# A graph layer on one core: gathered groups placed by a table of cycles, and the addition of b2 to x moved behind the last block multiply

## The chip, the core and the metric

The kernel runs on one core of one Trainium2 chip. The core has a matrix engine (TensorE, PE in the profile; its weight loads are the rows PEld), a vector engine (DVE), a scalar engine (ACT), GpSimd (POOL), a sync engine whose queue issues transfers (SP), and 16 DMA engines. The metric is the device time of one execution in microseconds, smaller is better. TensorE has two clock levels, 1.2 and 2.4 GHz; the profile calls them 0.5 and 1.0 of full speed.

## What is computed

N = 3125 nodes with 128 features, E = 53125 edges sorted by destination. Cut to what matters:

```python
msg = x[src] + edge_attr                                  # 53125 x 128
neigh = segment_sum(msg, dst, 3125)
rst = (1 + eps) * x + neigh
h = rst @ W1 + b1                                         # 3125 x 256
h = relu((h - mean(h)) * rsqrt(var(h) + 1e-5) * gamma + beta)   # over the nodes
out = layernorm(x + h @ W2 + b2)                          # over the features
```

## The kernel before

The edges are cut into G = 208 groups of 256 consecutive edges (two per partition). As `dst` is sorted, a group touches a window of at most 20 nodes. For every group the edge features are summed into `aggT`, the transposed node sums: two fp32 products of the edge rows with a 0/1 matrix `hit_c` or `hit_g` of 20 columns (L649, written in the trace as four matmuls), and an addition of the 20 columns by DVE (L983). The trace has 832 matmuls of L649: four for each group.

The sum of `x[src]` is made in two ways.

- **Counted groups** (`GROUPS_C` = 156, m = 0 to 155). TensorE makes a table of how often a source feeds a destination: `hit_l` and `hit_k`, made by DVE (`hits_k`, L904 to L910, 16 bit), are multiplied in `counts_a` and `counts_b` (L670, L673, L679), and ACT stores the product into `cnt` (L488). Later, x in three bf16 parts is multiplied with columns of `cnt` (`multiply`, L641). The destinations are cut into nine blocks (`BLOCKS_C`; 114, 180, 256, 376, 468, 466, 302, 120 and 110 columns), each multiplied by 75 matmuls, here called units. A block can be multiplied when its last group's counts are stored. `units(w)` spreads the 75 units of a block evenly over the windows until the next block is ready (`READY`); the last block's 75 come after all windows.
- **Gathered groups** (NG = 52, n = 0 to 51). SP loads the edge rows into one of 7 slots of `egat` (`slot`, L332), then POOL issues two indirect transfers which add the rows `x[src]` to it (`gather`, L402, called in L423), 104 in all. PE waits for both (`slot_gathered`, L694), and then needs no table for this group.

PE handles the groups one after another, in windows w = 0 to 207 (L683). What a window holds is fixed when the program is built: `in_window(w)` makes every fourth one gathered (w = 3, 7, ..., 207), and `C_AT`, `G_AT`, `C_OF` and `G_OF` are the two lists of windows and their inverses. PE, DVE, ACT and SP all follow this one order; POOL goes through n = 0 to 51 on its own, and waits for nothing but the edge rows of its slot. A slot is loaded again when its window has been summed (`window_summed`). In the first 24 counted groups (`KEEP`) PE makes two extra products into the same bank, which are overwritten (L665). In the first nine windows `turn_x` transposes x as well.

Behind its gathers POOL adds b2 to all of x (L429), one instruction over 128 x 3200 elements. PE reads the result in L730, behind the 14 products with W1 (`hidden`, L595), which follow the last block's multiply. From there on the statistics over the nodes, the scaling, the products with W2 (L741), the layer norm and the output follow.

Of the kernel before, what the change touches and what calls it, by code (L numbers as in the profile page):

```python
# [38 lines left out]
SETTLE = 2  # L39
# [4 lines left out]
PARTS = 3  # L44
SPREAD = 2
X_RATE = 3
LATE = 14
BATCHES_G = 2
KEEP = 24


def gnn_layer(nc, x, src, dst, edge, eps, w1, b1, gamma, beta, w2, b2, out):
# [4 lines left out]
    NT = -(-N // P)  # L57
# [6 lines left out]
    G = 2 * Q  # L64
    GL = E - (G - 1) * GROUP
    T = G * ROWS
    GC = GROUPS_C
    NG = G - GC
    QC = GC // 2
    HJ = 2 * ROWS  # L70
    F = len(BLOCKS_C)
    ENDS = [sum(BLOCKS_C[:f + 1]) for f in range(F)]
# [6 lines left out]
    SIZES = [hi - lo for lo, hi in zip(STARTS, STARTS[1:] + [CNT])]  # L79
# [1 line left out]
    KEYS_B = NT * WIN_B  # L81
    KEYS = NT * WIN

    def in_window(w):
        return (w + 1) * NG // G > w * NG // G

    C_AT = [w for w in range(G) if not in_window(w)]
    G_AT = [w for w in range(G) if in_window(w)]
    C_OF = {w: m for m, w in enumerate(C_AT)}
    G_OF = {w: n for n, w in enumerate(G_AT)}  # L90
    READY = [C_AT[g - 1] + SETTLE for g in ENDS[:-1]] + [G]
    UNITS = NT * PARTS

    def units(w):
        for f in range(F - 1):
            if READY[f] <= w < READY[f + 1]:
                n, i = READY[f + 1] - READY[f], w - READY[f]
                return f, UNITS * i // n, UNITS * (i + 1) // n
        return 0, 0, 0

    EARLY = STARTS[-1] // BANK
    KB = -(-GC // CARRY)
    assert D == P and H == HH * P and 0 < GL and Q <= P and QW - QL <= GL and GC % 2 == 0 and ENDS[-1] == GC
    assert KEYS <= BANK and max(SIZES) <= BANK and C_AT[0] == 0 and G_AT[-1] == G - 1 and GC % CHUNK == 0
    assert NG > SLOTS and 4 * (NB - 1) + 1 == NT
# [10 lines left out]
    with ExitStack() as ctx:  # L116
# [3 lines left out]
        def sem(name):  # L120
            return ctx.enter_context(nc.semaphore(name))

        big = sb("big", [P, NT * CNT // 2])
        at = [0]
# [126 lines left out]
        block_multiplied = sem("block_multiplied")  # L251
# [129 lines left out]
        @block.gpsimd  # L381
        def _(pool):
            nc.gpsimd.memset(xN[:, NT - 1, :], 0.0).then_inc(x_padded, 1)
            nc.gpsimd.iota(ident[:, :], [[1, P]], base=0, channel_multiplier=-1,
                           allow_small_or_imprecise_dtypes=True).then_inc(constants_made, 1)
            nc.gpsimd.memset(ones[:, :], 1.0).then_inc(constants_made, 1)
            nc.gpsimd.iota(spot[:, :], [[1, 2]], base=0, channel_multiplier=2,
                           allow_small_or_imprecise_dtypes=True).then_inc(constants_made, 1)
            nc.gpsimd.iota(pads[:, :], [[1, ROWS]], base=0, channel_multiplier=ROWS,
                           allow_small_or_imprecise_dtypes=True).then_inc(constants_made, 1)  # L390
            nc.gpsimd.iota(iota_w[:, :, :], [[0, BATCH * ROWS], [1, WIN]], base=0, channel_multiplier=0,
                           allow_small_or_imprecise_dtypes=True).then_inc(constants_made, 1)
            nc.gpsimd.iota(iota_k[:, :], [[1, KEYS_B + FROM_B]], base=0, channel_multiplier=0,
                           allow_small_or_imprecise_dtypes=True).then_inc(constants_made, 1)
            nc.gpsimd.iota(iota_c[:, :, :], [[0, CARRY], [1, NT]], base=1, channel_multiplier=0,
                           allow_small_or_imprecise_dtypes=True).then_inc(constants_made, 1)
            pool.wait_ge(path_known, 1)
            flag = pool.value_load(wide[0:1, 0:1], min_val=0, max_val=1)

            def gather(to, ix, op=ALU.bypass):  # L400
                pool.sem_inc(gather_released, 1)
                return nc.gpsimd.indirect_dma_start(to, None, x[:, :], bass.IndirectOffsetOnAxis(ap=ix, axis=0),  # L402
                                                    compute_op=op)

            with pool.If(flag != 0):
                nc.gpsimd.iota(iota_b, [[1, BANK]], base=0, channel_multiplier=0,
                               allow_small_or_imprecise_dtypes=True).then_inc(gen_iota_made, 1)
                pool.wait_ge(gen_sources_made, 1)
                with pool.Fori(0, G) as g:
                    pool.wait_ge(gen_messages_made, g * 2)  # L410
                    nc.gpsimd.tensor_copy(idx[:, 0:ROWS],
                                          src_all[:, bass.ds(g * ROWS, ROWS)]).then_inc(gen_indices_staged, 1)
                    pool.wait_ge(gen_indices_staged, g + 1)
                    for j in range(ROWS):
                        gather(grow[:, j, :], idx[:, j:j + 1]).then_inc(gen_rows_gathered, 16)
                    pool.wait_ge(gen_rows_gathered, g * 32 + 32)
            with pool.Else():
                for n in range(NG):
                    k = n % SLOTS
                    pool.wait_ge(slot_loaded[k], 16 * (n // SLOTS) + 16)  # L420
                    for j in range(ROWS):
                        m = n * ROWS + j
                        gather(egat[:, k, j * D:(j + 1) * D], srci[:, m:m + 1], ALU.add).then_inc(slot_gathered[k], 16)  # L423
                pool.wait_ge(x_rest_made, NB)
                pool.wait_ge(x_first_made, NB)

            pool.wait_ge(x_turned, NB)
            pool.wait_ge(b2_ready, 2)
            nc.gpsimd.tensor_tensor(xN[:, :, :], xN[:, :, :], b2e[:, 0:D].unsqueeze(1).to_broadcast([P, NT, D]),  # L429
                                    ALU.add).then_inc(x_b2_added, 1)  # L430
# [100 lines left out]
        def _(pe):  # L531
# [93 lines left out]
            with pe.Else():  # L625

                def multiply(f, u0, u1):

                    for u in range(u0, u1):
                        t, n = u // PARTS, u % PARTS  # L630
                        if f == 0 and u % (4 * PARTS) == 0:
                            pe.wait_ge(x_first_made, t // 4 + 1)
                            pe.wait_ge(x_middle_made, t // 4 + 1)
                            pe.wait_ge(x_last_made, t // 4 + 1)
                        if u == 0:
                            pe.wait_ge(counts_stored, ENDS[f])
                            if f < 2:
                                pe.wait_ge(x_scaled, NB)
                            if f >= 2:
                                pe.wait_ge(block_added, f - 1)  # L640
                        last = nc.tensor.matmul(ps[:, ACC + f % 2, 0:SIZES[f]], xp[:, t, n, :],  # L641
                                                cnt[:, t, STARTS[f]:STARTS[f] + SIZES[f]], start=(u == 0),
                                                stop=(u == UNITS - 1), skip_group_check=True)
                        if u == UNITS - 1:
                            last.then_inc(block_multiplied, 1)
# [12 lines left out]
                def counts_a(m):  # L658

                    pe.wait_ge(key_hits_made, m + 1)  # L660
                    if m >= BANKS_C:
                        pe.wait_ge(counts_stored, m - BANKS_C + 1)
                    if m < KEEP:
                        for n in range(2):
# [17 lines left out]

                for w in range(G):  # L683
                    f, u0, u1 = units(w)
                    ua = u0 + (u1 - u0 + 1) // 2
                    multiply(f, u0, ua)
# [29 lines left out]
                    if w in C_OF:  # L716
                        counts_b(C_OF[w])
                        multiply(f, ua, u1)
                multiply(F - 1, 0, UNITS)
                pe.wait_ge(counts_stored, GC)  # L720
# [25 lines left out]
        def _(dve):  # L746
# [129 lines left out]
            with dve.Else():  # L876
# [6 lines left out]
                def hits_c(b):  # L883

                    if b >= BATCHES:
                        dve.wait_ge(window_summed, C_AT[BATCH * (b - BATCHES + 1) - 1] + 1)
                    hits(b * BATCH, min(BATCH, GC - b * BATCH), hit_c[:, b % BATCHES, :, :]).then_inc(chunk_hits_made, 1)

                def hits_g(b):

                    if b >= BATCHES_G:
                        dve.wait_ge(window_summed, G_AT[BATCH * (b - BATCHES_G + 1) - 1] + 1)
                    hits(GC + b * BATCH, min(BATCH, NG - b * BATCH), hit_g[:, b % BATCHES_G, :, :]).then_inc(slot_hits_made, 1)
# [64 lines left out]
                for w in range(G + LAG):  # L958
# [38 lines left out]
                    if w == SPREAD * NB:  # L997
                        dve.wait_ge(lo_turned, 1)
                        dve.wait_ge(src_turned, 1)
                        nc.vector.memset(cnt[:, :, CNT - SPARE:CNT], 0.0).then_inc(spare_zeroed, 1)  # L1000
                    if w - 1 in READY[1:F]:
                        add_block(READY.index(w - 1) - 1, w - LAG + 1)
                        dve.wait_ge(block_added, READY.index(w - 1))
                        if READY.index(w - 1) == F - 1:
                            nc.vector.memset(tick[:, 1:2], 0.0).then_inc(sums_complete, EARLY)
# [73 lines left out]
```

## Time and profile before

| | us |
|---|---|
| Median of 3 runs | 280.7 (280.33 to 281.25) |
| The profiled execution, its own time | 281.48 |
| Its span, first to last instruction | 279.7 |
| PE busy, x2211 | 244.9 |
| DVE busy, x916 | 208.4 |
| POOL busy, x117 | 181.2 |
| ACT busy, x236 | 131.7 |
| Mean granted TensorE clock | 0.964 |

The sums are each engine's busy time over the span. The median is 0.8 us under the profiled execution's own time, and the span 1.8 us under it. Stages of the span: to 16 us the indices are prepared; from 16.2 to 239.8 us run the 208 windows; to 243.3 us the last block; to 254.0 us the products with W1; the rest is the normalisation and the output.

### The profile page before, as it was taken

Reading aid. Unit: us, or ns where it says so; the run is one execution under the profiler, and the core shown is the slowest. Engines: PE = TensorE matmul, PEld = TensorE weight load, DVE = VectorE, ACT = ScalarE, POOL = GpSimd, SP = SyncE. Lnnn points to the kernel's source line nnn. Section 1 sums busy time; section 2 is a strip of 40 time slices with the busy share of each in tenths; the row PEclk is TensorE's granted clock in tenths of the full one; section 3 lists DMA queues with packets and bytes.
Section 4 is the critical chain, followed back from the end, with each engine's and each line's share of the span. In section 5 each row is a group of like instructions: output and inputs, shape, how many; then the busy total and the mean of one; then the engine's idle time right before and its main releaser. Section 6 shows DMA issues by size and latency. Waiting matters only on the chain.

```text
span 279.7 us, 7102 instructions
## 1 busy us (share of the span) xinstructions
PE 244.9 (88%) x2211; PEld 200.6 (72%) x2211; DVE 208.4 (75%) x916; ACT 131.7 (47%) x236; POOL 181.2 (65%) x117
## 2 busy tenths in 40 slices
PE   1567989999998889988899999999999859999970
PEld 1456768899987677766788888777878648844870
DVE  3888997788998778778489887876867861178990
ACT  0327864455555535545255544444443302086494
POOL 2078888888888888888888888888888920000000
PEclk9999999999999999999599999999999968999995
DMA  5955766687888777788488888776665200000033
GB/s 165 285 172 108 147 145 137 156 191 197 189 195 185 178 164 171 181 179 183 96 172 192 174 195 171 167 179 145 150 126 105 53 2 0 2 0 1 2 114 116
DMA packets 49535, 38.39 MB, mean 137 GB/s; under 512 B 5083, under 2 KB 48523, under 8 KB 49497
## 3 DMA queue, kind: packets, MB, share of 16 engines
q1 hardware_dynamic: 32829, 30.62, 38.2%
q0 software_dynamic: 14976, 6.82, 20.4%
q10 hardware_dynamic: 1692, 0.48, 0.9%
q8 instruction: 19, 0.31, 0.5%
q14 instruction: 19, 0.16, 0.2%
HBM read 36.31 MB, written 1.60 MB: 136 GB/s over the span
## 4 chain that ended last, share of the span: by engine, by line
PE 46%; DMA 16%; issue 14%; POOL 9%; DVE 7%; ACT 4%; SPq 2%; DVEq 0%; ACTq 0%; POOLq 0%
PE ps L641 18%; PE ps L649 12%; DMA egat<-in_x_dram,srci 9%; POOL egat L402 9%; DMA egat<-in_edge_attr_dram 7%; PE ps L679 5%; PE ps L673 4%; PE ps L595 4%; ACT big L527 3%; PE ps L665 2%; SPq L321 1%; DVE big L1033 1%; DVE big L1035 1%; PE ps L670 1%; DVE hit_l L904 1%
## 5 line engine op out<-in xcount | busy, mean ns | idle before, releaser
L402 POOL DMA_INDIRECT egat<-in_x_dram,srci x104 | 172.2, 1656 | 44.0 <-issue 29.2
L488 ACT ACTIVATE big<-ps 128x500 f32 x156 | 95.1, 610 | 119.8 <-PE ps L679 91.6
L641 PE MATMUL ps<-big,xp 128*128 128x114 f16 (+8 forms) x675 | 116.9, 280 | 0.2 <-issue 0.2
L649 PEld LDWEIGHTS ps<-hit_c,ebuf 128*128 128x128 f32 x624 | 101.8, 194 | 16.6 <-DVE aggT L983 6.1
L649 PE MATMUL ps<-hit_c,ebuf 128*128 128x20 f32 x624 | 95.1, 230 | 9.1 <-DVE aggT L983 5.0
L641 PEld LDWEIGHTS ps<-big,xp 128*128 128x128 bf16 x675 | 63.0, 110 | 14.6 <-issue 1.1
L983 DVE TENSOR_TENSOR aggT<-aggT,ps 128x20 f32 x208 | 35.8, 172 | 49.8 <-PE ps L649 39.7
L910 DVE TENSOR_TENSOR hit_k<-iota_k,key 128x400 f16<-128x400 f16 x156 | 56.1, 359 | 0.0
L904 DVE TENSOR_TENSOR hit_l<-iota_k,lo 128x256 f16<-128x256 f16 x156 | 52.1, 334 | 1.7 <-issue 1.6
L679 PE MATMUL ps<-hit_k,hit_l 128*128 128x400 f16 x156 | 52.3, 335 | 0.0
L908 DVE TENSOR_TENSOR hit_k<-iota_k,key 128x300 f16<-128x300 f16 x156 | 48.2, 309 | 0.0
L673 PE MATMUL ps<-hit_k,hit_l 128*128 128x300 f16 x156 | 45.8, 294 | 0.0
L649 PEld LDWEIGHTS ps<-hit_g,egat 128*128 128x128 f32 x208 | 33.2, 196 | 17.6 <-DVE aggT L983 7.9
L649 PE MATMUL ps<-hit_g,egat 128*128 128x20 f32 x208 | 32.6, 242 | 9.6 <-DMA egat<-in_x_dram,srci 7.9
L670 PE MATMUL ps<-hit_n,hit_l 128*128 128x25 f16 x155 | 28.6, 185 | 0.0
L679 PEld LDWEIGHTS ps<-hit_k,hit_l 128*128 128x128 f16 x156 | 28.2, 181 | 0.1
L670 PEld LDWEIGHTS ps<-hit_n,hit_l 128*128 128x128 f16 x155 | 26.7, 172 | 1.8 <-issue 0.2
L673 PEld LDWEIGHTS ps<-hit_k,hit_l 128*128 128x128 f16 x156 | 15.1, 97 | 2.0 <-issue 0.4
L505 ACT ACTIVATE big<-ps,col 128x512 f32<-128x512 f32 (+1 forms) x14 | 8.6, 633 | 9.0 <-PE ps L595 8.9
L665 PE MATMUL ps<-iota_k 128*128 128x400 f16 x48 | 12.7, 348 | 0.0
L880 DVE TENSOR_TENSOR hit_c<-iota_w,rel 128x160 f32<-128x160 f32 x39 | 12.4, 318 | 0.0
L741 PE MATMUL ps<-w_sb,big 128*128 128x128 f32 (+1 forms) x100 | 11.6, 276 | 0.0
(101 smaller groups left out, 165.5 us busy)
## 6 DMA issues: line engine op xcount, KB each, us to landing
ebuf<-in_edge_attr_dram SPq DMA_DIRECT2D x78, 256.0 KB
egat<-in_edge_attr_dram SPq DMA_DIRECT2D x51, 128.0 KB
egat<-in_x_dram,srci POOLq DMA_INDIRECT x104
out_dram<-big SPq DMA_DIRECT2D x6, 256.0 KB
w_sb<-in_L_gnn_W_dram ACTq DMA_DIRECT2D x2, 128.0 KB, 6.8
rows<-in_dst_dram SPq DMA_DIRECT2D x1, 192.0 KB
rows<-in_src_dram ACTq DMA_DIRECT2D x1, 192.0 KB
egat<-in_edge_attr_dram SPq DMA_DIRECT2D x1, 66.0 KB
```

Of the source, the lines that this page charges most:

```text
L402: return nc.gpsimd.indirect_dma_start(to, None, x[:, :], bass.IndirectOffsetOnAxis(ap=ix, axis=0), compute_op=op)
L488: nc.scalar.activation(cnt[:, :, bass.ds(lows[m % LOADS], WIN)], ps[:, m % BANKS_C, 0:KEYS].rearrange("p (t n) -> p t n", n=WIN), ACT.Copy ...
L641: last = nc.tensor.matmul(ps[:, ACC + f % 2, 0:SIZES[f]], xp[:, t, n, :], cnt[:, t, STARTS[f]:STARTS[f] + SIZES[f]], start=(u == 0), stop= ...
L649: last = nc.tensor.matmul(ps[:, SUMS + w % BANKS_S, 0:WIN], rows_v[:, j * D:(j + 1) * D], hits_v, start=(j == 0), stop=(j == ROWS - 1))
L665: nc.tensor.matmul(ps[:, m % BANKS_C, 0:KEYS_B], iota_k[:, 0:P], iota_k[:, 0:KEYS_B], start=True, stop=True, skip_group_check=True)
L670: nc.tensor.matmul(counted(m)[:, :, 0], hit_l[:, (m - 1) % RING_K, 1, :], hit_n[:, (m - 1) // CARRY % 2, (m - 1) % CARRY, :], start=True, ...
L673: nc.tensor.matmul(counted(m)[:, :, 0:WIN_A], hit_l[:, m % RING_K, 0, :], hit_k[:, m % RING_K, 0:KEYS_A].rearrange("p (t n) -> p t n", n=W ...
L679: nc.tensor.matmul(counted(m)[:, :, FROM_B:WIN], hit_l[:, m % RING_K, 1, :], hit_k[:, m % RING_K, KEYS_A:KEYS_A + KEYS_B].rearrange("p (t ...
L904: nc.vector.tensor_tensor(hit_l[:, r, :, :].rearrange("p j (n two) -> p j n two", two=2), pairs(iota_k[:, 0:P]).unsqueeze(1).to_broadcast( ...
L908: nc.vector.tensor_tensor(pairs(hit_k[:, r, 0:KEYS_A]), pairs(iota_k[:, 0:KEYS_A]), key[:, 2 * m:2 * m + 1, :].to_broadcast([P, KEYS_A // ...
L910: nc.vector.tensor_tensor(pairs(hit_k[:, r, KEYS_A:KEYS_A + KEYS_B]), pairs(iota_k[:, FROM_B:FROM_B + KEYS_B]), key[:, 2 * m + 1:2 * m + 2 ...
L983: nc.vector.tensor_tensor(to, to, ps[:, SUMS + v % BANKS_S, 0:WIN], ALU.add).then_inc(window_added, 1)
```

## The change

The order of windows is no longer every fourth one. `arrange` walks over the windows with an account of cycles `now`. A window is made gathered once `now` has reached `GATHER_FIRST + n * GATHER` = 10200 + 9360 n; the last window is always gathered. The account is charged 670 cycles for a gathered window; for a counted one 670 + 770 (+ 810 in the first 24), but at least `HITS` = 2400; for each unit of a block its columns + 14; and 1680 while x is transposed. As the blocks' places depend on the order, this is repeated 12 times. `share` and `spans` are `units` and `READY` as before, written as functions of the order.

Besides, POOL waits for `block_multiplied` to reach F = 9, the end of the last block's multiply, before it adds b2 to x. The instructions themselves are the same, in kind and number.

```diff
+ROUNDS = 12
+SUM = 670
+COUNT = 770
+KEPT = 810
+HITS = 2400
+TURN = 1680
+GAP = 14
+GATHER = 9360
+GATHER_FIRST = 10200
...
-    def in_window(w):
-        return (w + 1) * NG // G > w * NG // G
-
-    C_AT = [w for w in range(G) if not in_window(w)]
-    G_AT = [w for w in range(G) if in_window(w)]
+    UNITS = NT * PARTS
+
+    def spans(c_at):
+
+        return [c_at[g - 1] + SETTLE for g in ENDS[:-1]] + [G]
+
+    def share(ready, w):
+
+        for f in range(F - 1):
+            if ready[f] <= w < ready[f + 1]:
+                n, i = ready[f + 1] - ready[f], w - ready[f]
+                return f, UNITS * i // n, UNITS * (i + 1) // n
+        return 0, 0, 0
+
+    def arrange():
+
+        order = [(w + 1) * NG // G > w * NG // G for w in range(G)]
+        for _ in range(ROUNDS):
+            ready = spans([w for w in range(G) if not order[w]])
+            now, m, n, order = 0, 0, 0, []
+            for w in range(G):
+                gathered = n < NG - 1 and w < G - 1 and (m == GC or now >= GATHER_FIRST + n * GATHER)
+                gathered = gathered or w == G - 1
+                f, u0, u1 = share(ready, w)
+                own = SUM if gathered else max(SUM + COUNT + KEPT * (m < KEEP), HITS)
+                now += own + (u1 - u0) * (SIZES[f] + GAP) + TURN * (X_RATE * w < NT)
+                order.append(gathered)
+                m, n = m + (not gathered), n + gathered
+            short = NG - sum(order)
+            at = [w for w in range(G) if not order[w]]
+            for w in at[len(at) - short:] if short > 0 else []:
+                order[w] = True
+        return order
+
+    IN_WINDOW = arrange()
+    C_AT = [w for w in range(G) if not IN_WINDOW[w]]
+    G_AT = [w for w in range(G) if IN_WINDOW[w]]
...
                 pool.wait_ge(x_first_made, NB)
+                pool.wait_ge(block_multiplied, F)
```

Worked out, the gathered windows are now w = 3, 6, 8, 12, 17, 20, 24, 28, 31, 35, 39, 42, 46, 50, 53, 57, 61, ..., 164, 168, 171, 175, 178, 181 and then 207: 51 of the 52 stand in the first 182 windows, one in 3.57, where it was one in 4; before, 45 stood there. The 466-column block was spread over windows 168 to 194 and is now over 175 to 197; the 302-column block over 195 to 205 and now over 198 to 205.

The place of group n = 50, on PE. Before it is window 203; its row is the one that waits for `slot_gathered1`, and `hit_c` rows are counted windows:

```order
L649 MATMUL ps<-hit_g,egat 128x20 [waits slot_gathered1,window_added]
L641 MATMUL ps<-big,xp 128x302 x3
L649 MATMUL ps<-hit_g,egat 128x20
L641 MATMUL ps<-big,xp 128x302 x4
L649 MATMUL ps<-hit_c,ebuf 128x20 [waits window_added]
L670 MATMUL ps<-hit_n,hit_l 128x25 [waits counts_stored,key_hits_made]
```

Now, as window 181, with L686 and L678 for what were L649 and L641:

```order
L686 MATMUL ps<-hit_g,egat 128x20 [waits slot_gathered1,window_added]
L678 MATMUL ps<-big,xp 128x466
L686 MATMUL ps<-hit_g,egat 128x20
L678 MATMUL ps<-big,xp 128x466 x2
L686 MATMUL ps<-hit_c,ebuf 128x20 [waits window_added]
L707 MATMUL ps<-hit_n,hit_l 128x25 [waits counts_stored,key_hits_made]
```

The group stood beside units of the 302-column block, four windows from the end; it now stands beside units of the 466-column block, with 26 windows behind it. Those are 25 counted ones and the last gathered one. From window 181 on PE has 56 units of 466 columns, 75 of 302, 75 of 120 and 75 of 110; from window 183 on it had, before, 18 counted and 7 gathered windows and 34, 75, 75 and 75 units.

POOL's last instructions, before and now (the gathers are those of n = 51):

```order
L402 DMA egat<-in_x_dram,srci 128x128
L417 UNCONDITIONAL_BRANCH [waits x_first_made,x_rest_made]
L429 TENSOR_TENSOR xN<-xN,b2e 128x3200 [waits b2_ready,x_turned]
```

Now:

```order
L438 DMA egat<-in_x_dram,srci 128x128
L453 UNCONDITIONAL_BRANCH [waits block_multiplied,x_first_made,x_rest_made]
L466 TENSOR_TENSOR xN<-xN,b2e 128x3200 [waits b2_ready,x_turned]
```

Nothing moved but the wait: the addition comes after the last block's multiply instead of right behind the last gather, and no instruction of POOL is queued behind it.

## Rows read from the trace of the kernel before

**Rows 1.** Source L402, count, ns min/median/max, first, last start; waits

```profile
L402 POOL DMA_INDIRECT egat<-in_x_dram,srci x104: 1545/1569/4465, 15.3 to 217.3; - x104
...
  DMA egat<-in_edge_attr_dram: 14.8, 8
...
  PE ps L649: 7.9, 9
```

**Rows 2.** Source L402 up to 64.8 us

```profile
L402 POOL DMA_INDIRECT egat<-in_x_dram,srci x24: 1545/1654/4465, 15.3 to 63.2; - x24
```

**Rows 3.** Timeline of POOL: start us, us, instruction, idle before it

```profile
97.66 1.55 POOL L402 DMA_INDIRECT egat<-in_x_dram,srci  x1 [0.30 <-issue]
...
112.83 1.55 POOL L402 DMA_INDIRECT egat<-in_x_dram,srci  x1 [0.30 <-issue]
...
127.98 1.54 POOL L402 DMA_INDIRECT egat<-in_x_dram,srci  x1 [0.30 <-issue]
...
213.57 1.54 POOL L402 DMA_INDIRECT egat<-in_x_dram,srci  x1 [0.30 <-issue]
```

**Rows 4.** Timeline of PE: three gathered windows that waited for their gathers

```profile
102.17 0.37 PE L649 MATMUL ps<-hit_g,egat 128*128 128x20 f32 x2 [1.13 <-DMA egat<-in_x_dram,srci]
...
116.77 0.37 PE L649 MATMUL ps<-hit_g,egat 128*128 128x20 f32 x2 [0.57 <-DMA egat<-in_x_dram,srci]
...
133.55 1.01 PE L649 MATMUL ps<-hit_g,egat 128*128 128x20 f32 x4 [1.85 <-DMA egat<-in_x_dram,srci]
```

**Rows 5.** Source L649 up to 200.2 us: matmuls of gathered windows

```profile
L649 PE MATMUL ps<-hit_g,egat x180: 180/266/382, 24.2 to 196.4; 128*128 128x20 f32 x180
```

**Rows 6.** Timeline of PE: start of windows 181, 183, 184, 185, 186

```profile
197.85 0.29 PE L649 MATMUL ps<-hit_c,ebuf 128*128 128x20 f32 x2
...
200.22 0.29 PE L649 MATMUL ps<-hit_g,egat 128*128 128x20 f32 x2
...
201.09 0.29 PE L649 MATMUL ps<-hit_c,ebuf 128*128 128x20 f32 x2
...
202.27 0.29 PE L649 MATMUL ps<-hit_c,ebuf 128*128 128x20 f32 x2
...
203.26 0.29 PE L649 MATMUL ps<-hit_c,ebuf 128*128 128x20 f32 x2
```

**Rows 7.** Timeline of PE: windows 197 and 198 begin, 197's units

```profile
215.62 0.32 PEld L649 LDWEIGHTS ps<-hit_c,ebuf 128*128 128x128 f32 x2
...
216.35 1.06 PE L641 MATMUL ps<-big,xp 128*128 128x302 f16 x7
...
217.12 0.32 PEld L649 LDWEIGHTS ps<-hit_c,ebuf 128*128 128x128 f32 x2
```

**Rows 8.** The chain in order of time: start us, us, what

```profile
236.47 1.94 PE ps L641 x37
...
239.80 3.63 PE ps L641 x75
243.43 10.38 PE ps L595 x24
```

**Rows 9.** Timeline around POOL's addition

```profile
218.06 7.95 DVE L904 TENSOR_TENSOR hit_l<-iota_k,lo 128x256 f16<-128x256 f16 x1
...
218.30 7.55 POOL L429 TENSOR_TENSOR xN<-xN,b2e 128x3200 f32<-128x3200 f32 x1
...
226.65 0.62 PE L649 MATMUL ps<-hit_c,ebuf 128*128 128x20 f32 x2 [3.72 <-DVE aggT L983]
```

**Rows 10.** Stages: five engines' busy us (x), granted clock, DMA share, GB/s

```profile
134.00:141.00 7.00, 7.00 (x42) 5.97 (x43) 3.84 (x18) 1.78 (x3) 5.88 (x4) 0.55 0.59 109
...
227.00:235.00 8.00, 8.00 (x56) 6.27 (x56) 2.02 (x12) 1.70 (x3) 0.00 (x0) 0.66 0.01 2
```

**Rows 11.** Timeline behind the last block: first statistics, then L730

```profile
245.17 1.49 DVE L1013 BATCH_NORM_STATS2 big<-big 128x6 f32<-128x512 f32 x2 [1.24 <-ACT big L505]
...
254.04 2.37 PE L730 MATMUL ps<-xN,ident 128*128 128x512 f32 x5
```

More of the change, by code:

```diff
@@ L82, in gnn_layer @@
     KEYS = NT * WIN
-    def in_window(w):
-        return (w + 1) * NG // G > w * NG // G
-    C_AT = [w for w in range(G) if not in_window(w)]
-    G_AT = [w for w in range(G) if in_window(w)]
+    UNITS = NT * PARTS
[28 more added lines that the diff above has]
+    G_AT = [w for w in range(G) if IN_WINDOW[w]]
     C_OF = {w: m for m, w in enumerate(C_AT)}
     G_OF = {w: n for n, w in enumerate(G_AT)}
-    READY = [C_AT[g - 1] + SETTLE for g in ENDS[:-1]] + [G]
-    UNITS = NT * PARTS
+    READY = spans(C_AT)
     def units(w):
[L95 to L99, printed above, removed]
+        return share(READY, w)
     EARLY = STARTS[-1] // BANK
```

## The prediction

> **What bounds the kernel now.** I read the sources of the waits first, then POOL's timeline beside PE's, then the price of one window. The kernel has two streams that meet in the gathered windows. POOL's stream is one indirect transfer after the other: the median issue is 1.57 us, the shortest of 104 is 1.545 us [rows 1], 0.30 us of idle stands ahead of each [rows 3], and the first starts at 15.3 us, the last at 217.3 [rows 1]: 202.0 us for 103 steps, 1.96 us a gather and 3.92 us a group. 103 pairs of issue and gap at the median fill 193 of the 202 us, so at most 9 us in it can be waits for edge rows or longer issues (the 14.8 us of waits for edge rows [rows 1] lie mostly ahead of the first gather). POOL runs at its own pace from end to end. PE waits for it only 7.9 us, in 9 cases [rows 1].
>
> How late a gather is when its issue ends: the second gather of three groups ended at 99.21, 114.38 and 129.52 us [rows 3], and the windows that waited for them started at 102.17, 116.77 and 133.55 [rows 4]: 3.0, 2.4 and 4.0 us. I take 2.9.
>
> PE's stream: window 184 (counted, 3 units of 466 columns) takes 202.27 - 201.09 = 1.18 us, window 185 (counted, 2 units) 0.99, window 183 (gathered, 3 units) 0.87 [rows 6]. So a 466-column unit is 0.19 to 0.20, a counted window's own work 0.60 and a gathered one's 0.28 us. Window 197 takes 1.50 us with 7 units of 302 columns [rows 7]: 0.129 a unit. The 120-column ones take 1.94 / 37 = 0.052, the 110-column ones 3.63 / 75 = 0.048 [rows 8].
>
> **The change, first part: the order.** The account that places the groups charges a counted window at least 2400 cycles, which is 1.00 us at 2.4 GHz, and then its units on top. The rows say 0.60 us and the units on top. For the 132 counted windows behind the first 24 that is 0.40 us too much each, 53 us in all. The account therefore believes PE to be slower than it is, and thinks the gathers have landed at windows that PE reaches long before. Group 50 is put where the account reads 10200 + 50 x 9360 = 478,200 cycles, 199 us after the first window, and that is window 181. In the trace PE is at window 181 at 197.85 us [rows 6], 182 us after the first window, and this although it waited for gathers on the way. The group's second gather is the last but two of all; it starts at 213.57 and ends at 215.11 [rows 3]. With 2.9 us to land, window 181 can't start before 218.0. Before, the group had window 203, behind all this.
>
> Can PE keep up with POOL until then, or is it late itself? The place where the two meet comes early. Group 11 is in window 42 now; its second gather is the 24th, issued at about 64.8 us [rows 2] and landed at 67.7. From there to 218.0 are 150.3 us. In windows 42 to 180 PE has 100 counted windows (60.0 us), 39 gathered ones (10.9) and 40, 75, 75, 75 and 19 units of 180, 256, 376, 468 and 466 columns, which at their columns over 2.4 GHz, as the two measured sizes cost, are 3.0 + 8.0 + 11.8 + 14.6 + 3.7 = 41.1 us: 112 us in all. So PE will wait some 38 us there, less what it loses otherwise (DVE's additions, the clock). It is bound by the gathers in nearly every gathered window from 42 to 181, not in 9.
>
> From window 181 on nothing waits for gathers (the last lands about 221, for window 207). What is left is PE's: 25 counted windows x 0.60 = 15.0; 2 gathered x 0.28 = 0.6; 56 x 0.195 = 10.9; 75 x 0.129 = 9.7; 75 x 0.052 = 3.9; 75 x 0.048 = 3.6: 43.7 us. The last block ends at 218.0 + 43.7 = 261.7 us.
>
> I test this sum on the kernel before. 180 of the gathered matmuls, 45 windows, lie ahead of 200.2 us [rows 5], so the gathered one at 200.22 is window 183. From there its 18 counted and 7 gathered windows and 34, 75, 75 and 75 units give 10.8 + 2.0 + 6.6 + 9.7 + 3.9 + 3.6 = 36.6 us, and with the 3.7 us of the stall below the end would be at 240.5. It was at 243.4 [rows 8], and the missing 2.9 us are the low clock of the next paragraph. The prices hold.
>
> **Second part: the addition of b2.** It takes 7.55 us from 218.30. DVE's 16-bit comparison, begun just before, took 7.95 us in place of the usual 0.3; PE then ran out of additions and stood 3.72 us [rows 9]. Behind this standstill the granted clock was 0.66 in the mean from 227 to 235 us [rows 10], that is some 5.4 us at 1.2 GHz, which cost 2.7 us. Moved, it costs no stall among the windows, and the sum above has none. Saved: 3.7 + 2.9 = 6.6 us, all of it inside the 43.7 already.
>
> In its new place it starts with the products with W1, at what was 243.3 us, and must be done before L730, which was at 254.04 [rows 11]: 10.7 us of cover for 7.6, so it costs nothing for PE. Beside it DVE adds the last block, writes a small tile that releases the products with W1 (L1008), and makes the statistics (L1013, 0.7 us each, released by ACT) [rows 11]. No row shows such an instruction beside a POOL instruction that reads SBUF. At best they run on: 0. At worst they stand until POOL is through: the products from the ninth on are released 0.7 us late, and fourteen statistics then need 14 x 0.6 = 8 us from 251 on, instead of ending with the last store at 255.5: 3.6 us late, 4 in all. The row of the comparison is nearest in engine, yet it has two SBUF inputs and these have one; I take 0 and keep 4 as the bound.
>
> The Trainium skill (SBUF — State Buffer, section Who interferes with whom) says that a DVE instruction with two SBUF inputs contends with a GpSimd instruction that reads SBUF, and one with a single SBUF input outside the two-port modes does not. The trace agrees in its one case, the 7.95 us; by the rule the statistics go on and the cost is 0.
>
> **The sum.** The profiled execution had its last block done at 243.4; now 261.7, 18.3 us later. What follows keeps its length. Span 279.7 + 18.3 = 298.0, own time 281.48 + 18.3 = 299.8, and against the median of 280.7: 299.0.
>
> **Rivals.**
>
> *Gathers come quicker (7 in 100).* PE and DVE stand more, and POOL's issues could all be at the shortest one, 1.545 + 0.30 = 1.85 us. From the 24th to the 102nd gather that is 78 x 1.85 = 144.3 us, instead of 215.1 - 64.8 = 150.3: 6.0 us less, 293. For it: long issues do occur. Against: the median of 1.57 is nearly there, and DVE has just as many comparisons to make.
>
> *The clock falls (14 in 100).* The trace shows the granted clock at 0.55 from 134 to 141 us [rows 10], behind the wait of 1.85 us [rows 4]. With PE idle a quarter of the time, such a fall may come often. One costs some 3.4 us (7 us at half). PE has 38 us in hand, so that some ten falls are hidden behind the gathers; but one in the last groups before window 181, where a period's work (2.5 counted windows and a gathered one, 3 units each, some 4 us) leaves nothing, comes on top, and constant falls from window 42 on would eat all in hand. 302 to 306. Against: waits of 1.13 and 0.57 us [rows 4] were not followed by a fall at once.
>
> The Trainium skill (TensorE: Matmul & The Clock Gate, section HAM oscillation) tells of a kernel whose waits for transfers between short bursts of matmuls brought the low clock back in every round. Here that would be this rival at its upper end.
>
> *The statistics stand behind POOL (5 in 100).* 4 us, as bounded above: 303.
>
> *Not slower (3 in 100).* The one way: POOL's stream is not its own limit but follows PE's demand, so that group 50 lands where PE arrives. It decides from 18.3 us earlier on, (150.3 - 18.3) / 78 = 1.69 us a gather, idle included; faster only below that, for instance 1.65 gives 280.7 - 78 x 0.04 = 277.6. Against it stand all 104 rows: none is under 1.545 + 0.30 = 1.85 us, and its waits for free slots are few. That PE doesn't follow the account's order at all is excluded by the rows of the order. 279.
>
> **The numbers.** Forecast 299.0 with 71 in 100; its own range 295 to 302 (landing 2.4 to 4.0 us, prices of windows 2% off, a fall partly shown). Range with the rivals: 292 to 305. A measurement of this kernel can't tell less than 0.3% from no change. Faster 2%, within 0.3% 1%, slower 97%.
>
> **What would show it.** Right: PE's waits for gathers grow from 7.9 us to about 30, in 30 or more cases; the 102nd gather starts near 213.6 and window 181 near 218; no wait from there to the last block's end near 261.7; the DVE comparison of 8 us is gone; the addition of b2 runs beside the products with W1, and L730 doesn't wait. Wrong: gathers steadily below 1.85 us apart; window 181 before 212; PE's waits for gathers below 15 us; the granted clock at half for more than 60 us; a statistics instruction of 7 us beside the addition.

## The result, and the profile after

The changed kernel takes 297.7 us (median of 4 runs, 297.2 to 298.1) against 280.5 for the kernel before (4 runs, 277.4 to 281.3): ratio 1.064, 95% interval 1.055 to 1.072. Slower, as forecast; 299.0 was predicted. The profiled execution has a span of 295.9 us, 16.2 more than before.

The source of the gathers in the changed kernel, columns as in [rows 1] (L438 is what was L402, L686 what was L649, L678 what was L641):

```profile
L438 POOL DMA_INDIRECT egat<-in_x_dram,srci x104: 1545/1546/4716, 15.2 to 215.4; - x104
...
  issue: 30.8, 101
  DMA egat<-in_edge_attr_dram: 13.2, 3
...
  PE ps L686: 17.0, 17
```

POOL's stream is almost the one of before: its last gather starts at 215.4 us where it was 217.3. PE's waits for it went from 7.9 us in 9 cases [rows 1] to 17.0 in 17. The chain of work that ended last, as shares of the span, shows the same from the end's side: the gathers' issues on POOL make up 9% of it before and 25% now. By line, the first line is the kernel before, the second the changed one:

```profile
PE ps L641 18%; PE ps L649 12%; DMA egat<-in_x_dram,srci 9%; POOL egat L402 9%; DMA egat<-in_edge_attr_dram 7%; PE ps L679 5%; PE ps L673 4%; PE ps L595 4%; ACT big L527 3%; PE ps L665 2%; SPq L321 1%; DVE big L1033 1%; DVE big L1035 1%; PE ps L670 1%; DVE hit_l L904 1%
POOL egat L438 25%; PE ps L678 12%; PE ps L686 6%; DMA egat<-in_x_dram,srci 6%; DMA egat<-in_edge_attr_dram 4%; PE ps L632 4%; ACT big L564 3%; PE ps L716 3%; PE ps L710 2%; SPq L357 1%; DVE big L1070 1%; DVE big L1072 1%; PE ps L615 1%; DVE big L1081 1%; PE ps L702 0%
```

The three places of the prediction, in the timeline of the changed kernel: window 42, the second gather of group 50 (the 102nd), and window 181, which waited for it:

```profile
67.16 0.37 PE L686 MATMUL ps<-hit_g,egat 128*128 128x20 f32 x2 [0.30 <-DMA egat<-in_x_dram,srci]
...
211.50 1.74 POOL L438 DMA_INDIRECT egat<-in_x_dram,srci  x1 [0.30 <-issue]
...
216.01 0.37 PE L686 MATMUL ps<-hit_g,egat 128*128 128x20 f32 x2 [1.17 <-DMA egat<-in_x_dram,srci]
```

The issue of the 102nd gather ended at 211.50 + 1.74 = 213.24 us (215.11 before [rows 3]) and window 181 started 2.8 us later, at 216.0, where it was at 197.9 [rows 6]. From there PE has no gap. Stages of the changed kernel, columns as in [rows 10]: from window 42 to 181, the four stretches around a fall of the clock, and from window 181 to the last block's end:

```profile
67.20:216.00 148.80, 133.57 (x1140) 110.78 (x1141) 103.68 (x491) 60.78 (x101) 125.04 (x79) 0.90 0.71 156
74.00:88.00 14.00, 14.00 (x91) 12.53 (x89) 7.83 (x38) 4.79 (x8) 11.87 (x8) 0.51 0.61 123
108.00:112.00 4.00, 4.00 (x31) 3.45 (x30) 2.22 (x12) 1.84 (x3) 3.39 (x3) 0.57 0.63 140
128.50:139.00 10.50, 10.50 (x59) 9.10 (x60) 5.31 (x24) 3.02 (x5) 8.98 (x6) 0.51 0.58 116
179.50:183.50 4.00, 4.00 (x22) 2.95 (x20) 2.35 (x12) 1.38 (x3) 3.39 (x3) 0.57 0.70 141
216.00:259.60 43.60, 43.59 (x463) 35.82 (x464) 22.42 (x101) 15.62 (x25) 0.94 (x1) 1.00 0.21 58
```

The last stage is PE without a gap at full clock: 43.6 us, where 43.7 were summed. In the first, PE is idle for 148.8 - 133.6 = 15.2 us, and the mean clock of 0.90 costs it another 15 (10% of 148.8).

Behind the last block, timeline of the changed kernel: the products with W1, the addition of b2 in its new place, the tile that releases the last products, a statistic, and the first read of x with b2:

```profile
259.51 2.80 PE L632 MATMUL ps<-aggT,w_sb 128*128 128x512 f32 x6
...
260.09 6.98 POOL L466 TENSOR_TENSOR xN<-xN,b2e 128x3200 f32<-128x3200 f32 x1 [43.16 <-PE ps L678]
260.11 0.06 DVE L1045 MEMSET tick<- 128x1 f32 x1
...
261.41 0.69 DVE L1050 BATCH_NORM_STATS2 big<-big 128x6 f32<-128x512 f32 x1 [1.24 <-ACT big L542]
...
270.28 1.94 PE L767 MATMUL ps<-xN,ident 128*128 128x512 f32 x4
```

The addition ends at 267.1 us, 3.2 before it is needed. Beside it the DVE instructions run at their usual length, 0.06 and 0.69 us; from the first product with W1 to the read of x it is 10.8 us (259.51 to 270.28), as before (243.27 to 254.04 [rows 11]).

### The profile page after: what moved, and what is told of

Its sections match the earlier page's. It is cut to its first block, busy times and chain, and to the rows that moved or that the text cites. A ratio compares the mean times of both kernels' runs of the same rounds, so it can differ in the third digit from the quotient of the medians.

```text
span 295.9 us, 7101 instructions
## 1 busy us (share of the span) xinstructions
PE 256.6 (87%) x2211; PEld 208.0 (70%) x2211; DVE 203.5 (69%) x916; ACT 131.9 (45%) x236; POOL 179.3 (61%) x117
## 4 chain that ended last, share of the span: by engine, by line
PE 28%; POOL 25%; issue 23%; DMA 10%; DVE 5%; ACT 4%; SPq 2%; POOLq 0%; ACTq 0%; DVEq 0%
POOL egat L438 25%; PE ps L678 12%; PE ps L686 6%; DMA egat<-in_x_dram,srci 6%; DMA egat<-in_edge_attr_dram 4%; PE ps L632 4%; ACT big L564 3%; PE ps L716 3%; PE ps L710 2%; SPq L357 1%; DVE big L1070 1%; DVE big L1072 1%; PE ps L615 1%; DVE big L1081 1%; PE ps L702 0%
## 5 line engine op out<-in xcount | busy, mean ns | idle before, releaser
L438 POOL DMA_INDIRECT egat<-in_x_dram,srci x104 | 170.3, 1638 | 44.0 <-issue 30.8
L678 PE MATMUL ps<-big,xp 128*128 128x114 f16 (+8 forms) x675 | 118.6, 285 | 0.2
L686 PEld LDWEIGHTS ps<-hit_c,ebuf 128*128 128x128 f32 x624 | 107.3, 204 | 13.3 <-issue 4.8
L686 PE MATMUL ps<-hit_c,ebuf 128*128 128x20 f32 x624 | 99.0, 237 | 5.5 <-issue 4.1
L678 PEld LDWEIGHTS ps<-big,xp 128*128 128x128 bf16 x675 | 63.8, 110 | 16.4 <-issue 3.0
L716 PE MATMUL ps<-hit_k,hit_l 128*128 128x400 f16 x156 | 54.5, 350 | 0.0
L686 PEld LDWEIGHTS ps<-hit_g,egat 128*128 128x128 f32 x208 | 32.7, 204 | 27.6 <-issue 17.9
L686 PE MATMUL ps<-hit_g,egat 128*128 128x20 f32 x208 | 33.2, 252 | 17.5 <-DMA egat<-in_x_dram,srci 17.0
L710 PE MATMUL ps<-hit_k,hit_l 128*128 128x300 f16 x156 | 47.4, 304 | 0.0
L941 DVE TENSOR_TENSOR hit_l<-iota_k,lo 128x256 f16<-128x256 f16 x156 | 44.5, 285 | 1.7 <-issue 1.6
L466 POOL TENSOR_TENSOR xN<-xN,b2e 128x3200 f32<-128x3200 f32 x1 | 7.0, 6978 | 43.2 <-PE ps L678 43.2
L716 PEld LDWEIGHTS ps<-hit_k,hit_l 128*128 128x128 f16 x156 | 29.6, 190 | 0.0
L707 PEld LDWEIGHTS ps<-hit_n,hit_l 128*128 128x128 f16 x155 | 27.9, 180 | 1.9 <-issue 0.4
L710 PEld LDWEIGHTS ps<-hit_k,hit_l 128*128 128x128 f16 x156 | 15.3, 98 | 2.1 <-issue 0.5
```

Source lines behind the costliest of these rows:

```text
L686: last = nc.tensor.matmul(ps[:, SUMS + w % BANKS_S, 0:WIN], rows_v[:, j * D:(j + 1) * D], hits_v, start=(j == 0), stop=(j == ROWS - 1))
L707: nc.tensor.matmul(counted(m)[:, :, 0], hit_l[:, (m - 1) % RING_K, 1, :], hit_n[:, (m - 1) // CARRY % 2, (m - 1) % CARRY, :], start=True, ...
L710: nc.tensor.matmul(counted(m)[:, :, 0:WIN_A], hit_l[:, m % RING_K, 0, :], hit_k[:, m % RING_K, 0:KEYS_A].rearrange("p (t n) -> p t n", n=W ...
L716: nc.tensor.matmul(counted(m)[:, :, FROM_B:WIN], hit_l[:, m % RING_K, 1, :], hit_k[:, m % RING_K, KEYS_A:KEYS_A + KEYS_B].rearrange("p (t ...
L941: nc.vector.tensor_tensor(hit_l[:, r, :, :].rearrange("p j (n two) -> p j n two", two=2), pairs(iota_k[:, 0:P]).unsqueeze(1).to_broadcast( ...
```

## The experiments

Theory: the new order asks for the gathered groups earlier than POOL's stream delivers them, since its account charges a counted window 1.00 us where the trace has 0.60; the moved addition by itself is a gain. Rivals: the moved addition costs; the falls of the clock cost; PE's own work in the new order costs; any order is bound by POOL. Each run has runs of the kernel before measured beside it: their median is 279.6 us for the first four kernels and 280.7 for the last three. The changed kernel was not measured again beside them; what is compared with its 297.7 us is compared across measurements, whose medians of the kernel before differ by 1.1 us.

### The addition alone

```diff
 # the order of before
                 pool.wait_ge(x_first_made, NB)
+                pool.wait_ge(block_multiplied, F)
```

> The order of before, with only the addition of b2 moved behind the last block's multiply. Theory (the new order alone makes the change slow, the moved addition is a gain): the stall of 3.7 us behind POOL's addition and the 2.9 us of low clock after it go, nothing takes their place: 280.6 - 6.6 = 274 us, ratio 0.975 to 0.98; the longest DVE comparison is near 0.4 us, the last block ends near 237. Rival (the addition in its new place holds up the products or statistics behind the last block, or the stall is only moved): 278 to 281 us. Rival (PE was waited for by something else in that stretch): a wait of another kind stands at 218 to 230 us, and the time is within 1 us of before.

Measured: 274.7 us against 279.6, ratio 0.983 (0.975 to 0.990). Stages of this kernel over the place of the old stall, those of 218 to 227 and, as in [rows 10], 227 to 235 us:

```profile
218.00:227.00 9.00, 9.00 (x96) 7.61 (x95) 2.96 (x14) 3.10 (x5) 0.00 (x0) 1.00 0.05 7
227.00:235.00 8.00, 8.00 (x149) 7.90 (x146) 0.77 (x5) 0.68 (x1) 0.00 (x0) 1.00 0.01 2
```

PE is busy all through, at full clock, where it stood for 3.72 us [rows 9] and then ran at 0.66 [rows 10]. The moved addition is a gain of 4.9 us, clear of no change, though a gain of 2% isn't shown; the 6.6 predicted are inside the interval (2.7 to 7.0 us). Both rivals fall.

### The order alone

```diff
 # the new order
                 pool.wait_ge(x_first_made, NB)
-                pool.wait_ge(block_multiplied, F)
```

> The new order, without the wait of POOL for the last block. Theory: group 50 still lands near 216, so window 181 starts as in the changed kernel; the addition starts near 217 us and stops DVE for 7 us, PE stands 3 to 4 us and the granted clock falls behind it: 297.7 + 6.6 = 304 us (302 to 306). Rival (the moved addition is what made the change slower): 281 us or less. Rival (in the new order the stall is covered, since PE has counted windows only): 298.

Measured: 303.9 us, ratio to before 1.085 (1.076 to 1.095), the changed kernel's being 1.064. Timeline of this kernel:

```profile
214.87 7.77 DVE L940 TENSOR_TENSOR hit_l<-iota_k,lo 128x256 f16<-128x256 f16 x1
214.95 7.53 POOL L465 TENSOR_TENSOR xN<-xN,b2e 128x3200 f32<-128x3200 f32 x1
...
223.28 0.62 PE L685 MATMUL ps<-hit_c,ebuf 128*128 128x20 f32 x2 [4.55 <-DVE aggT L1019]
```

The stall of [rows 9] is back, in the counted windows behind window 181. So the order alone costs more than the whole change, and the counted windows don't cover the stall. Window 181 starts at 213.96 us in this kernel, 2 us before that of the changed one, so the added time stands behind it. Loss of the order and gain of the addition add up within the intervals: 303.9 - 279.6 = 24.3 for the first, -4.9 for the second, 19.4 against 17.2 measured for both. In the new order the moved addition is worth 303.9 - 297.7 = 6.2 us.

### Half the gathers, in the new order

```diff
-                    for j in range(ROWS):
+                    for j in range(1):
                         m = n * ROWS + j
                         gather(egat[:, k, j * D:(j + 1) * D], ...)
...
-                        pe.wait_ge(slot_gathered[k], 32 * (n // SLOTS) + 32)
+                        pe.wait_ge(slot_gathered[k], 16 * (n // SLOTS) + 16)
```

> The changed kernel with one indirect transfer for each gathered group instead of two: the rows of the second edge of each partition get no x added (left out), PE waits for one. Instructions of the other engines and the order are the same. Theory (POOL's stream of gathers sets the pace from window 42 to 181): with 1.9 us a group it binds nothing; PE's waits for gathers go below 2 us, the 150 us from window 42 to 181 shrink to PE's own 112 us plus 6 to 12 us of other waits; the last block ends near 228, time 262 to 270 us. Rival (the low clock, or the order of PE's own work with 25 counted windows in a row, makes the change slow): 290 us or more.

This kernel leaves out x for half of the gathered edges, so its output is not that of the reference; it only shows where the time goes. Measured: 266.3 us, ratio 0.951 (0.943 to 0.959). All waits of PE for another engine or a transfer in this kernel:

```profile
PE ps L573 <- DMA row<-in_L_gnn_eps_dram: 6.2, 1, 6.2
PE ps L686 <- DVE hit_c L917: 4.1, 1, 4.1
PE ps L686 <- DVE aggT L1020: 3.9, 5, 1.4
PE ps L578 <- ACT big L493: 1.3, 1, 1.3
```

Not one for a gather. Window 181 starts here (timeline of this kernel) 31.4 us before that of the changed one:

```profile
184.59 0.29 PE L686 MATMUL ps<-hit_g,egat 128*128 128x20 f32 x2
```

Stages of this kernel, columns as in [rows 10]: from its window 42 (67.86 us) to its window 181, and from there to the last block's end:

```profile
67.86:184.59 116.73, 115.42 (x1144) 100.60 (x1141) 101.44 (x493) 61.03 (x101) 58.01 (x36) 1.00 0.69 173
184.59:228.20 43.61, 43.61 (x464) 35.83 (x463) 22.83 (x103) 15.91 (x26) 0.00 (x0) 1.00 0.20 60
```

PE's instructions and their order are those of the changed kernel, and it is 31 us quicker. The first stage takes 116.7 us instead of 148.8, the second 43.6 in both. So the loss is the waiting for POOL's stream; 25 counted windows in a row, and the units moved beside them, took no longer than their sum. This kernel also moves less data; the next one has all 104 gathers and the same time, so that isn't the cause.

### The account with 1440 cycles

```diff
-HITS = 2400
+HITS = 1440
```

> The changed kernel with the least price of a counted window at 1440 cycles instead of 2400 (0.60 us at 2.4 GHz, what the trace shows). The gathered windows are then 3, 6, 9, 13, 17, ..., one in about four, the last at 195, 197, 200, 203, 205, 206, 207. Theory (the account's price of a counted window is the error): PE is no longer bound by gathers for long, waits for them below 8 us, last block near 227 to 232, time 264 to 270 us, below both kernels. Rival (any order that puts windows behind the gathers' landing costs as much, since POOL is the bound of the whole kernel): 280 or more.

Measured: 267.0 us, ratio 0.955 (0.947 to 0.962). PE's waits for gathers in this kernel, and from its timeline window 207, which waits for the last gather:

```profile
PE ps L686 <- DMA egat<-in_x_dram,srci: 3.7, 3, 1.9
```

```profile
223.07 0.37 PE L686 MATMUL ps<-hit_g,egat 128*128 128x20 f32 x2 [0.28 <-DMA egat<-in_x_dram,srci]
```

One number of the account, put to what the trace shows, turns a loss of 17 us into a gain of 13. The cause is the price of a counted window, and the rival that any order is bound by POOL at 280 us or more falls.

### A filler product in the groups before window 181

```diff
-                    if m < KEEP:
-                        for n in range(2):
+                    if m < 130:
+                        for n in range(2 if m < KEEP else 1):
                             nc.tensor.matmul(ps[:, m % BANKS_C, 0:KEYS_B], ...)
```

> The changed kernel with one extra product of 400 columns, overwritten, in counted groups 24 to 129 (the first 24 have two as before): about 0.17 us each, 18 us more work for PE, all of it ahead of window 181, so that the granted clock falls less often. Theory (PE has some 38 us in hand there, and the falls of the clock are hidden behind the gathers): the time stays at 297.7 within 1.5 us, window 181 starts at 215 to 217.5; PE's idle time shrinks. Rival (the four falls of the granted clock, 10 to 14 us of lost work, are what makes the change slow): with fewer falls 288 to 292 us. Rival (PE is the bound there): 18 us slower, 310 to 316.

Measured: 296.7 us, ratio to before 1.059 (1.051 to 1.067); the changed kernel has 1.064. The same stage, window 42 to 181, of this kernel, its window 181, and PE's waits for gathers:

```profile
67.20:215.70 148.50, 139.80 (x1251) 111.95 (x1250) 104.40 (x493) 61.45 (x102) 124.73 (x79) 0.98 0.72 156
```

```profile
215.66 0.29 PE L686 MATMUL ps<-hit_g,egat 128*128 128x20 f32 x2
```

```profile
PE ps L686 <- DMA egat<-in_x_dram,srci: 10.7, 17, 1.8
```

Some 100 of the 106 extra products lie in this stage, and it is as long as without them: 148.5 us against 148.8. The mean clock rises from 0.90 to 0.98, that is 12 us of PE's time won back; PE's idle time falls from 15.2 to 8.7 us; together that pays for the some 17 us of filler, and window 181 now starts without a wait. So PE had about this much time in hand, and it is used up here. Had PE been the bound, 17 us more work less the 12 won back would have made the kernel some 5 us slower.

That more work and a higher clock change together leaves this run alone short of a proof about the clock. The four runs of the changed kernel itself say more: their mean clocks were 0.942, 0.948, 0.954 and 0.977, and their times 297.75, 298.11, 297.2 and 297.7 us. The first and the last differ by 0.035 in the clock, some 10 us of PE's time, and by 0.05 us in the time. The falls of the clock are not the cause.

### All three numbers after the trace

```diff
-HITS = 2400
+HITS = 1440
-GATHER = 9360
-GATHER_FIRST = 10200
+GATHER = 9300
+GATHER_FIRST = 20300
```

> The changed kernel with the account after the trace in all three numbers: least price of a counted window 1440, first landing 20300 cycles (21.75 us end of issue + 2.9 - 16.2 us), 9300 a group. Gathered windows 6, 8, 12, 17, ..., 196, 199, 202, 204, 205, 206, 207. Theory: waits for gathers fall below those of the version with 1440 alone, by the 4 us that groups are placed later: 263 to 268 us, 0 to 3 us under that version. Rival (too late a place makes POOL wait for slots and shifts the last landings): last landing later than 221 us and no gain, or slower by up to 3 us.

Measured: 265.7 us, ratio 0.951 (0.941 to 0.961). PE waits for a gather once, for the last one; timeline of this kernel:

```profile
218.25 1.54 POOL L438 DMA_INDIRECT egat<-in_x_dram,srci  x1 [0.30 <-issue]
...
221.74 0.37 PE L686 MATMUL ps<-hit_g,egat 128*128 128x20 f32 x2 [1.37 <-DMA egat<-in_x_dram,srci]
```

It is the quickest of all, 1.3 us under the version with 1440 alone, but the two intervals overlap, so this order of the two is not shown. Stages of this kernel, columns as in [rows 10]:

```profile
60.00:100.00 40.00, 40.00 (x453) 36.62 (x452) 37.37 (x184) 23.67 (x39) 33.91 (x21) 1.00 0.83 194
100.00:140.00 40.00, 39.86 (x392) 34.66 (x390) 36.24 (x177) 22.40 (x37) 33.62 (x21) 1.00 0.84 193
```

PE is busy nearly all through these stretches at full clock, and it reaches the last gathered window 1.4 us before the gather has landed (221.7 us). So the two streams end together here: PE's own work is the next bound, and in this order less work for POOL could give no more than these 1.4 us. It fits that the kernel with half the gathers, which waits for none, takes 266.3 us as well. DVE is close behind, busy for 37.4 of the first 40 us.

### The old price with slower gathers in the account

```diff
-GATHER = 9360
+GATHER = 11500
```

> The changed kernel with the least price left at 2400 and the cycles for a group's gathers at 11500 instead of 9360, so that one error of the account makes up for the other: gathered windows 3, 6, 9, 15, 19, 24, 28, ..., 192, 195, 198, 201, 204, 207. Theory (only the distance of the gathered windows in PE's real time matters): 264 to 270 us, within 3 us of the version with 1440. Rival (the price of counted windows acts in another way than through the places of the gathered ones): over 275.

Measured: 267.8 us, ratio 0.955 (0.948 to 0.963). PE's waits for gathers in this kernel:

```profile
PE ps L686 <- DMA egat<-in_x_dram,srci: 6.8, 8, 1.2
```

A wrong price of the counted window does no harm when the distance of the gathered ones is stretched by as much (11500 / 9360 = 1.23). As far as these runs go, what counts is where the gathered windows stand in PE's real time.

## Why the prediction was right

**The price of a counted window** was the step on which all hung: 0.60 us in the rows against 1.00 in the account. The change of this number alone moved the time from 297.7 to 267.0, and the stretched gathers did the same by another way. Shown. One figure on the way is too large for what hangs on it: of the 132 counted windows with 0.40 us too much, 25 stand behind window 181, so the account was 107 x 0.40 = 43 us too high there, not 53. The run with half the gathers reaches window 181 at 184.59 us, 168 us after its first window, where the account said 199: 31 us. The other 12 are about what the account leaves out in that run, 8.0 us of waits for DVE and 3.6 us of low clock ahead of window 42. The sum of the prediction didn't use the 53 us.

What the prediction overlooked is where a price of 2400 cycles may come from. DVE's three comparisons for a counted group take 0.285 + 0.308 + 0.360 = 0.95 us, in the page of the changed kernel:

```profile
L947 DVE TENSOR_TENSOR hit_k<-iota_k,key 128x400 f16<-128x400 f16 x156 | 56.2, 360 | 0.0
L945 DVE TENSOR_TENSOR hit_k<-iota_k,key 128x300 f16<-128x300 f16 x156 | 48.1, 308 | 0.2
L941 DVE TENSOR_TENSOR hit_l<-iota_k,lo 128x256 f16<-128x256 f16 x156 | 44.5, 285 | 1.7 <-issue 1.6
```

So 1.00 us is near DVE's time for such a window, and PE does its units beside it; the account puts the units on top. That the price was meant so isn't on record, and an account that takes the larger of DVE's time and PE's time with the units was not tried.

**POOL's stream sets window 181.** Predicted at 218.0, measured at 216.0: the issues were at their shortest more often than before (median 1.546 us, was 1.569), and the 102nd gather ended 1.9 us sooner; it landed 2.8 us after its end, where I took 2.9. That the landing came so near is partly luck: in the same kernel the window that starts at 72.52 us waited for a gather that had ended its issue at 67.86, 4.7 us before, outside the 2.4 to 4.0 I had read. This is the small part of the rival of quicker gathers that came true, 2 of its 6 us. The run with half the gathers shows the mechanism.

**PE's work behind window 181**: 43.7 us predicted, 43.6 measured. The last block's end was to be 261.7 us and was 259.6, so the forecast is too high by the 2 us of POOL's stream. The forecast of 299.0 looks nearer than that, 1.3 us off, because it took off 0.8 us for the profiled execution before being above its median; after the change the two were equal (297.75 and 297.73). That part is luck.

**The moved addition**: no wait at L767, statistics and the small tile unhindered, so the zero in the sum was right and the bound of 4 us wasn't touched. The gain of removing the stall was put at 6.6 us and measured at 4.9 (2.7 to 7.0).

**The clock** fell in four stretches, 31 us in all, and cost nothing in the end, by the argument made for the time in hand; the four runs at different clocks and the filler show it. That none of it hit window 181 was not certain ahead: the fall near 180 to 183 us was made good by then, since window 181 itself still waited 1.17 us. The rival was rightly kept apart, and its price would have been on top.

**A miss** is the size of PE's waits for gathers, which I put at about 30 us in 30 or more cases and which are 17.0 in 17. In windows 42 to 181, 14 of the 40 gathered ones waited, not nearly all. The step that failed is that I gave all the 38 us in hand to these waits but for a few. The stage divides them otherwise: 148.8 us hold 112 of work by my prices, 15.2 of idle time, 15 lost at the low clock, and 6.6 that none of these hold. With half the gathers PE was busy for 115.4 us in this stage at full clock, so some 3.4 of the 6.6 are work that my prices put too low; some 3 stay open. A slow PE arrives late at a gathered window and doesn't wait. So the wait, read alone, shows half of the 31 us that half the gathers gave back, and the low clock hides most of the rest. The start of window 181, with its wait of 1.17 us, tells more than the sum of the waits.

That a faster version lay so near was not in the prediction. With the stall and the waits for gathers gone, the kernel before would have been at about 266, an estimate made afterwards from its own rows: 280.5 - 6.6 - 7.9. The corrected orders arrived there (265.7 to 267.8), and so did the kernel with half the gathers.

## What to carry to other kernels

An order worked out from a table of costs is as good as its largest entry: multiply each entry by its count and compare with the trace before using it; here 107 windows at 0.40 us too much were 43 us ahead of the place that decided. When two streams meet, work out where the slower one's last piece lands and how much of the other stream stands behind that place in the order: this sum (216 + 43.6) is the end, whatever the engines between show as busy. And where a stream is paced by another, neither a slower clock nor filler work costs anything until the time in hand is used up (here some 30 us), so a low clock seen there is not yet a cause.

## What the runs showed of the hardware

- Beside a POOL addition that reads and writes SBUF (7 us), DVE's batch-norm statistics with one fp32 input from SBUF took 0.69 us and a small memset 0.06, their usual times; a 16-bit comparison with two SBUF inputs took 7.77 to 7.95 us, where its mean is 0.285. The POOL addition itself took 6.98 us beside the first kind (6.97 in the run with the addition alone) and 7.53 to 7.55 beside the second.
- An indirect transfer of 128 rows of 512 bytes with addition costs POOL 1.545 us at the least in both kernels, and 0.30 us of idle stands ahead of it in the rows shown. Where PE waited for it, it landed 1.8 us (issue end 221.26, window 223.07, the account with 1440) to 4.7 us (67.86 and 72.52, the changed kernel) after the end of its issue.
- The granted clock fell to 1.2 GHz behind waits that I had thought short. In the changed kernel each of the four stretches in the table above came behind one wait of 1.52 to 2.15 us: that from 74 us on behind the first of these, that from 108 behind the second, that from 128.5 behind the third, that from 179.5 behind the last. The waits of 1.03 and 1.19 us which ended at 162.95 and 169.95 us were not followed by one.

```profile
72.52 0.37 PE L686 MATMUL ps<-hit_g,egat 128*128 128x20 f32 x2 [1.92 <-DMA egat<-in_x_dram,srci]
...
106.58 0.37 PE L686 MATMUL ps<-hit_g,egat 128*128 128x20 f32 x2 [2.15 <-DMA egat<-in_x_dram,srci]
...
128.24 0.37 PE L686 MATMUL ps<-hit_g,egat 128*128 128x20 f32 x2 [1.52 <-DMA egat<-in_x_dram,srci]
...
178.31 0.59 PE L686 MATMUL ps<-hit_g,egat 128*128 128x20 f32 x4 [2.14 <-DMA egat<-in_x_dram,srci]
```
